# The last two experts' rows reach the first token tile through a matmul with a one-hot matrix, and its reload waits for two scatters fewer

## The reference, cut to what matters

```python
x = x + _L0_ffn_ref(_layernorm(x), gate_w, w_gate, w_up, w_down)   # 64 experts, 8 of them for each token
x = x + _L1_xattn_ref(_layernorm(x), ctx, ctx, Wq, bq, Wk, bk, Wv, bv, Wo, bo)
```

## Time and profile before

| | us |
|---|---|
| median of 3 runs | 2289.22 |
| lowest and highest of them | 2286.27, 2293.53 |
| the profiled execution, its own time | 2283.12 |
| its span in the trace | 2281.3 |
| its mean granted clock of TensorE | 0.973 |

### The profile page before, as it was taken

The page is one execution under the profiler, slowest core; times in us unless marked ns, Lnnn a source line. Parts: engine busy times, 40 slices in busy tenths (PEclk is TensorE's granted clock), DMA queues, the critical chain, the costliest instruction groups (busy, mean ns, idle before and its releaser), DMA issues. The chain is left out here.

```text
span 2281.3 us, 48070 instructions
## 1 busy us (share of the span) xinstructions
PE 2170.7 (95%) x19023; PEld 1624.5 (71%) x19023; DVE 1116.2 (49%) x2940; ACT 330.8 (15%) x775; POOL 255.9 (11%) x298
## 2 busy tenths in 40 slices
PE   7999999999889999999996999999999999899798
PEld 6788878888668888888874676666765766556443
DVE  3665433434444444444433556565565555466623
ACT  0000011111111111111111122212121221112110
POOL 0000000000034334434420000000000000001102
PEclk9999999999889999999997999999999999999799
DMA  7234420000259999999994312313313215400134
GB/s 261 91 99 155 118 89 11 19 9 9 92 184 333 330 331 327 335 328 331 329 341 155 125 60 75 110 38 120 101 42 124 78 65 165 176 12 29 47 125 152
DMA packets 93504, 337.64 MB, mean 148 GB/s; under 512 B 16016, under 2 KB 16784, under 8 KB 84065
## 3 DMA queue, kind: packets, MB, share of 16 engines
q1 hardware_dynamic: 65312, 284.12, 34.8%
q0 software_dynamic: 16576, 39.50, 6.8%
q10 hardware_dynamic: 11520, 12.65, 1.8%
HBM read 286.39 MB, written 51.25 MB: 148 GB/s over the span
## 5 line engine op out<-in xcount | busy, mean ns | idle before, releaser
L628 PEld LDWEIGHTS psum<-work,arena 128*128 128x128 f32 x3072 | 355.2, 193 | 31.7 <-issue 30.8
L628 PE MATMUL psum<-work,arena 128*128 128x128 f32 x3072 | 355.8, 276 | 1.4 <-ACT work L1736 1.4
L392 PEld LDWEIGHTS psum<-work,arena 128*128 128x128 f32 x2560 | 293.4, 194 | 8.9 <-issue 8.4
L392 PE MATMUL psum<-work,arena 128*128 128x128 f32 x2560 | 294.8, 278 | 3.8 <-DMA arena<-in_q 2.6
L1868 POOL TENSOR_TENSOR small<-small 128x1 f32<-128x1 f32 x136 | 72.4, 532 | 1963.7 <-issue 892.5
L704 PE MATMUL psum<-work,arena 128*128 128x257 f32 x1024 | 234.4, 382 | 0.7 <-DVE arena L1378 0.7
L1611 ACT COPY work<-psum 128x512 f32<-128x512 f32 (+1 forms) x182 | 97.0, 547 | 799.0 <-PE psum L303 719.7
L704 PEld LDWEIGHTS psum<-work,arena 128*128 128x128 f32 x1024 | 190.8, 191 | 28.1 <-issue 1.2
L398 PE MATMUL psum<-arena,work 128*128 128x512 f32 x448 | 204.6, 609 | 0.7 <-ACT work L1611 0.7
L636 PE MATMUL psum<-arena,work 128*128 128x512 f32 x384 | 182.0, 610 | 2.0 <-DVE work L1329 2.0
L726 PE MATMUL psum<-work 128*128 128x512 f32 x384 | 169.2, 593 | 0.0
(11 more groups left out here) (214 smaller groups left out, 2274.9 us busy)
## 6 DMA issues: line engine op xcount, KB each, us to landing
arena<-in_experts SPq DMA_DIRECT2D x64, 2304.0 KB, 9.1
expert_rows<-work SPq DMA_DIRECT2D x8, 2304.0 KB, 10.8
work<-in_ctxT SPq DMA_DIRECT2D x32, 514.0 KB, 4.9
work<-in_ctx SPq DMA_DIRECT2D x32, 512.0 KB, 4.3
work<-in_ctx_tail SPq DMA_DIRECT2D x32, 450.0 KB, 3.5
work<-last_key_probs ACTq DMA_DIRECT2D x32, 256.0 KB, 4.3
arena<-in_experts SPq DMA_DIRECT2D x8, 1024.0 KB, 15.5
arena<-in_qkv SPq DMA_DIRECT2D x1, 6144.0 KB, 19.3
```

The lines of the kernel that those rows point to most:

```text
L392: done = nc.tensor.matmul(to[:, n * P:(n + 1) * P], w[:, j, at:at + P], src[:, j * P:(j + 1) * P], start=(j == 0), stop=(j == KD - 1))
L628: done = nc.tensor.matmul(to[:, n * P:(n + 1) * P], w[:, at:at + P], xgT[e % 2][:, j * P:(j + 1) * P], start=(j == 0), stop=(j == KD - 1))
```

## The change

The scatters of experts 62 and 63 no longer touch tile 0. For these two (`LATE` = 2), `answer` makes one matrix more on VectorE, `onehotT[n]`, which has a 1 where the slot's token is in tile 0 (tokens 0 to 127), and then sets the slot's address for the scatter out of bounds if it is in tile 0. TensorE multiplies these matrices with the two `y` buffers into one PSUM bank, after `down(63)`, and VectorE adds that to tile 0 after it has come back. SP loads tile 0 when 62 scatters have landed, and the four small loads are moved ahead of that wait. Before the context loads SP now waits for the two matmuls and for all 64 scatters. In the last round VectorE runs `silu_up(63)` ahead of `take_down(62)`.

```diff
+LATE = 2
+        onehotT = list(carve(work, 9216, *[CAP] * LATE))
@@ TensorE, experts_pe, behind the last eight
+            pe.wait_ge(s_onehotT, LATE)
+            for n in range(LATE):
+                pe.wait_ge(s_y_ready, EXPERTS - LATE + n + 1)
+                done = nc.tensor.matmul(bank[4], onehotT[n], y[n], start=(n == 0), stop=(n == LATE - 1))
+            done.then_inc(s_late, 1)
@@ VectorE, experts_dve
-            def answer(e, r):
+            def answer(e, r, late=False):
...
                 nc.vector.tensor_copy(gidx.bitcast(U32)[:, n:n + 1], fidx)
+                if late:
+                    nc.vector.tensor_tensor(fidx, fidx, empty, ALU.add)
+                    dve.drain()
+                    nc.vector.tensor_scalar(onehotT[n % LATE], iota128, fidx, None, ALU.is_equal).then_inc(s_onehotT, 1)
+                    nc.vector.tensor_scalar(empty, fidx, float(P), float(NOWHERE), ALU.is_lt, ALU.mult)
+                    dve.drain()
                 nc.vector.tensor_tensor(sidx.bitcast(U32)[:, n:n + 1], fidx, empty, ALU.add)
...
                 for e in range(ROUND):
-                    silu_up(e, r)
+                    if not (final and e == ROUND - 1):
+                        silu_up(e, r)
                     if not (final and e >= ROUND - 4):
                         ask(e + 4, r)
-                        answer(e + 4, r)
+                        answer(e + 4, r, final and e + 4 >= ROUND - LATE)
+                    if final and e == ROUND - 2:
+                        silu_up(e + 1, r)
                     take_down(e, r)
@@ VectorE, cross_dve
             dve.wait_ge(s_x_back[0], 16)
+            dve.wait_ge(s_late, 1)
+            nc.vector.tensor_tensor(x[:, 0:D], x[:, 0:D], bank[4], ALU.add)
             layernorm(dve, 0)
@@ SP
-            sp.wait_ge(s_scatter, 16 * EXPERTS)
-            sp.dma_start(x[:, 0:D], x_d[0:P, :]).then_inc(s_x_back[0], 16)
             load_row(bq1, "bq1", s_w["bias_q1"])
             sp.dma_start(ctx_last, t["ctx_last"]).then_inc(s_w["ctx_last"], 16)
             load_row(bk1, "bk1", s_w["bias1"])
             sp.dma_start(bv1, t["bv1"]).then_inc(s_w["bias1"], 16)
+            sp.wait_ge(s_scatter, 16 * (EXPERTS - LATE))
+            sp.dma_start(x[:, 0:D], x_d[0:P, :]).then_inc(s_x_back[0], 16)
+            sp.wait_ge(s_late, 1)
+            sp.wait_ge(s_scatter, 16 * EXPERTS)
```

More of the change, by code:

```diff
@@ L254, in build @@
         s_scatter = sem("scattered")
+        s_onehotT, s_late = sem("late_onehot_ready"), sem("late_rows_full")
         s_ctxT = [sem("ctx_columns_even"), sem("ctx_columns_odd")]
```

## The result

| | before | changed |
|---|---|---|
| median of 17 runs, us | 2290.57 | 2282.44 |
| lowest and highest | 2286.27, 2298.88 | 2278.15, 2290.39 |
| profiled execution, own time | 2283.12 | 2282.48 |
| its span | 2281.3 | 2280.7 |

The ratio is 0.9960, with a 95% interval of 0.9950 to 0.9969: the change gives 9.2 us (7.1 to 11.5, of 2290.57); the two medians by themselves are 8.1 us apart. 9.7 were forecast.

What follows compares the result with a forecast made beforehand. TensorE was taken as the bound, busy 95% of the span, with time to win where it idles before layer 1's cross attention. 10.5 - 0.8 = 9.7 us off the 2289.22 us median gave 2279.5 us, range 2273 to 2285.5.

Steps and rivals of the forecast that it cites:

- The chain: Between layer 0's experts and layer 1's cross attention: last scatters, tile 0's reload and layer norm leave TensorE idle until 1218.11.
- Step 1: End of the last round: take_down(63) starts at 1199.8 on scatter 61's landing, not at 1202.01 on TensorE; takes 0.75 us.
- Steps 2 to 4: Late matmuls, tile 0's load and addition: sum and load ready within a microsecond, layer norm at 1203.3, 10.5 us sooner.
- step 2: Late matmuls on TensorE: second follows take_down(63), 0.9 us at full clock, twice at low; sum in PSUM at 1201.7 to 1202.6.
- Step 5: Moved small loads on the DMA engines delay scatter 61 and tile 0's load by 0.8 us together; gain 9.7 us.
- step 4: VectorE's addition to tile 0 with its drain takes 0.8 us; layer norm starts at 1203.3 instead of 1213.81.
- Step 6: VectorE's extra work in two answers, 0.8 us each, is hidden behind take_down(58)'s 1.73 us scatter wait; costs nothing.
- step 7: Context loads, weights o and the other seven tiles still arrive in time, hidden by 10 us or more.
- Step 8: TensorE's restart at the transposes and query projection is slow as before; the low clock costs 3.1 us.
- The rival in which the clock helps: TensorE restarts at full clock after the shorter pause: gain 12.8 us, 2276 us; chance 0.13.
- the moved loads in the way: Small loads delay scatter 61 by 2.1 us and tile 0's load takes 5.0: gain 6.1 us, 2283 us; chance 0.17.
- the slow clock lasting over the keys' weights and scores: Low clock holds after TensorE's restart, 18.7 us more: kernel 9.0 us slower, 2298 us; chance 0.04.

Runs made afterwards that it cites:

- e4: Changed kernel with LATE = 1: only expert 63 goes through the matmul and tile 0's load waits for 63 scatters; ratio 0.9977 to before.
- e3: Kernel before with only VectorE's new order, silu_up(63) ahead of take_down(62); ratio 1.0002 to before.
- e12: Kernel before with only the four small loads moved ahead of the wait for the 64 scatters; ratio 0.9997 to before.
- e2: Changed kernel with VectorE's old order in the last round, silu_up(63) behind take_down(62); ratio 0.9960 to before.
- e1: Changed kernel with tile 0's load put back ahead of the four small loads; ratio 0.9946 to before.
- e6: Changed kernel with one more 512 KB load ahead of tile 0's load in SP's queue; one run, tile 0's load took 5.1 us.
- e9: Kernel before again, no edit, timed against itself; ratio 0.9996.
- e7: Changed kernel with tile 0's load ahead of the small loads and eight idle matmuls behind the two late ones; ratio 0.9953 to before.
- e11: Changed kernel with three experts through the matmul, a third y buffer, tile 0's load first and seven idle matmuls; ratio 0.9925 to before.
- e10: Changed kernel again, no edit, beside the kernel before for its profile; one run, layer norm 12.9 us from the start of scatter 61.
- e5: Changed kernel again, no edit, timed against the kernel before; ratio 0.9961.
- third series: Group of kernels timed together on one chip: both kernels again, the moved loads alone, and three late experts with idle matmuls; before's median 2275.88 us.

## Why the prediction was right

- **The chain** was read rightly. The gap was set by the last scatters and the reload, and the wait for fewer scatters moved it. e4 gives about 5 us for one scatter and the changed kernel about 9 for two; e3 and e12 show that neither of the other edits does anything by itself.
- **Step 1** (`take_down(63)` starts on scatter 61's landing) held, and e2 shows that it holds without the reordering too. The reordering saves TensorE a pause that nothing behind it depends on.
- **Steps 2 to 4**: the second late matmul ended 2.2 us before the load in the changed kernel, not within a microsecond of it, because the load was longer (in e1, where it took 2.6 us, they were 0.7 us apart). The 0.3 us from engine to engine in step 2 stands in no row; the changed trace has 0.06 from the end of `take_down(63)` to the late matmul. The slow `down(63)` that step 2 reads from the trace of before didn't come back in any other profile. The addition and its drain took 0.77 us.
- **Step 5** is the term that was mis-sized. The forecast took 0.8 us for scatter 61 and the load together. The load alone lost 0.8 to 1.4 us against 2.7 (four profiles, mean 1.1), and e1 and e6 show that the moved loads are the cause. Scatter 61 landed at 8.0 to 8.1 us in the changed kernel, where the trace of before had 7.3. That was a low value for before (e3, e9 and e12 have 8.0, 7.6 and 8.0), yet it isn't shown that the scatter loses nothing: the nine profiles in which the small loads were issued before it landed have 8.0 to 8.3 us, the five others (before, e1, e3, e7, e9) 6.4 to 8.0. So the layer norm came 12.6 us behind the start of scatter 61 (mean of four) where step 4 alone has 10.8: 1.1 us for the load and 0.7 for the scatter, 1.8 in place of 0.8. The forecast was nearer than that by luck, since the kernel before takes 21.7 us on average and not the 21.3 of the one trace that was read. Layer norm by layer norm, the four profiles with the old waits (21.3, 22.0, 21.7, 21.7) and the four with the new ones and the moved loads (13.0, 12.3, 12.2, 12.9) are 9.1 us apart, which fits the 9.2 us of the timed runs.
- **Step 6** (VectorE's extra work is hidden) and **step 7** (nothing is late next) held: the wait of `take_down(58)` shrank from 1.73 us to 1.08 and wasn't used up, and no wait on the context, on `o` or on the other tiles stands in the traces.
- **Step 8**: the restart was slow again, as forecast, and costs 2.8 us, not 3.1. The rival in which the clock helps didn't come true by the change. The profiles of e7 and e11 show that idle matmuls can bring it about in this stage; the timed runs of e7 don't confirm it.
- **The rivals**: the moved loads in the way came to about a third of their price (10.5 - 9.1 = 1.4 of 10.5 - 6.1 = 4.4 us); the slow clock lasting over the keys' weights and scores didn't happen in any profile.
- **The signs.** Of those given for being wrong one came: tile 0's load took 4.2 us, over 4, in the first profile of the changed kernel and in e10 (3.6 in e5). And what "would upset it all", a later stage of another length, was there in the first pair: the profiled execution was forecast at 2273.4 us and took 2282.48. In the third series, where both have the short length, the spans of e9 and e10 are 7.7 us apart.
- The forecast of 2279.5 us was 2.9 us under the median of 2282.44. 1.35 of these are the median of before, which was 2289.22 in three runs and 2290.57 in seventeen. The rest is the size of step 5 and the scatter of the runs.

## What to carry to other kernels

When serial transfers stand between two stages, find which rows the next stage needs first and let the last transfers miss them; a small matmul can carry these rows at the price of a wait that is already there. Look at what the moved load stands behind in its queue: 1 MB of loads that nobody needs yet cost it over a microsecond, and the order should be by when each is wanted. If TensorE must wait some microseconds before a dense stage, idle matmuls up to its restart are worth trying, for in two profiles here they gave back 2.8 us of low clock; but time them, since the one kernel with little else new (e7) wasn't clearly faster for it. And compare profiles by stage, since another stage's clock can hide a gain of this size.

## What the runs showed of the hardware that was not expected

- The self attention of layer 1 had two lengths, 194 to 199 us and 209 to 212 us, for the same instructions (mean granted clock 0.91 to 0.94, and 0.87 to 0.90). All profiles of one series had the same length, and two series on the same chip had different ones. The cause stays open.
- The load of bq1, issued right behind 6 MB of others, kept SP in its issue for 15.4 us (13.1 to 16.4 in the six other profiles that have it there); issued after the scatters a load of that size takes 0.4 (the context load in the earlier trace rows). That the queue was full is my reading and was not tried. What stands behind such an issue on SP waits with it.
- A scatter-add of 128 rows of 2 KB took 4.8 to 4.9 us from start to landing with the DMA engines free, and 6.4 to 8.3 us for scatter 61, which ran beside the projection weights.
- The transposes and the float32 projection ran at the full clock from their first instruction when idle matmuls had ended 0.6 to 0.7 us ahead of them (0.63 us for the four transposes against 1.09).
